# Residual stream kept turned by a reflection, with the normalisation computed inside the stages that make the stream

## What is computed

```
h = tokenizer(x)                                        # spectral features, one hidden layer, normalised
h = h + neighbourhood_attention(layernorm(h))
h = h + mixture_of_experts(layernorm(h))                # 8 experts, best 2 of them; itself residual: out = tokens + ...
h = h + decayed_attention(layernorm(h))
h = h + soft_experts(layernorm(h))                      # routing weights from mean over the batch of layernorm(h)
layernorm(h) = (h - mean(h)) / sqrt(var(h) + 1e-5)      # over the 64 channels of a token
```

## Time and profile before

| | before |
|---|---|
| median of 3 runs | 1049.62 us |
| the profiled execution | 1048.99 us, of which the span from first to last instruction is 1047.2 us |
| PE busy | 936.4 us (89%) |
| DVE busy | 583.4 us (56%) |
| ACT busy | 596.8 us (57%) |
| POOL busy | 174.8 us (17%) |
| DMA | 17.15 MB, mean 16 GB/s |
| mean granted TensorE clock | 0.967 of full speed |

### The profile page before, as it was taken

The page is one execution under the profiler, slowest core; times in us unless marked ns, Lnnn a source line. Parts: engine busy times, 40 slices in busy tenths (PEclk is TensorE's granted clock), DMA queues, the critical chain, the costliest instruction groups (busy, mean ns, idle before and its releaser), DMA issues. The chain is left out here.

```text
span 1047.2 us, 29479 instructions
## 1 busy us (share of the span) xinstructions
PE 936.4 (89%) x12388; PEld 447.7 (43%) x12388; DVE 583.4 (56%) x797; ACT 596.8 (57%) x822; POOL 174.8 (17%) x209
## 2 busy tenths in 40 slices
PE   3987969999999998864999999979999789999998
PEld 2331436667666766321222222337774422222222
DVE  3655346677676766246766755337874334444443
ACT  2998957676667676662444444662226545555543
POOL 1214131313131311034000000001113470000000
PEclk9998989999999999986999999989999899999999
DMA  2210000000000000000000000012210011211110
GB/s 53 28 27 0 1 2 4 5 4 4 4 4 5 4 4 4 2 1 0 1 2 1 1 1 1 1 30 52 52 32 1 0 31 41 58 45 42 41 41 31
DMA packets 27512, 17.15 MB, mean 16 GB/s; under 512 B 18753, under 2 KB 23010, under 8 KB 27394
## 3 DMA queue, kind: packets, MB, share of 16 engines
q1 hardware_dynamic: 26626, 14.16, 5.8%
q10 hardware_dynamic: 768, 1.23, 0.4%
HBM read 2.80 MB, written 4.19 MB: 7 GB/s over the span
## 5 line engine op out<-in xcount | busy, mean ns | idle before, releaser
L1585 DVE SCALAR_TENSOR_TENSOR se_a<-se_p,cols,z 128x1024 f32<-128x1024 f32 x64 | 82.2, 1284 | 118.9 <-PE se_p L1528 118.9
L1563 ACT ACTIVATE se_a<-se_p,cols 128x512 f32<-128x512 f32 x128 | 92.6, 773 | 79.8 <-PE se_p L1518 79.8
L1141 ACT ACTIVATE me_g<-me_p,cols 128x1024 f32<-128x1024 f32 x64 | 71.3, 1114 | 83.5 <-PE me_p L1095 83.4
L1232 DVE TENSOR_TENSOR me_gw<-me_pc,me_g 128x1024 f32<-128x1024 f32 x64 | 78.4, 1224 | 62.5 <-PE me_pc L1107 56.5
L991 DVE TENSOR_REDUCE na_rowmax<-na_ps 128x16 f32<-128x1024 f32 x64 | 78.0, 1219 | 54.0 <-PE na_ps L887 54.0
L801 POOL TENSOR_TENSOR z<-na_k,const 128x512 f32<-128x512 f32 x64 | 64.6, 1040 | 221.9 <-ACT na_k L940 221.9
L740 DVE TENSOR_TENSOR z<-ln_cen,ln_rstd 128x512 f32 (+1 forms) x64 | 44.3, 692 | 82.3 <-ACT ln_rstd L730 82.3
L896 PE MATMUL na_pt<-const,na_e 128*128 128x128 f32 x512 | 69.1, 278 | 14.2 <-ACT na_e L963 13.0
L994 DVE TENSOR_TENSOR na_e<-na_ps,na_rowmax 128x1024 f32<-128x1024 f32 x64 | 78.4, 1225 | 2.2
L1518 PE MATMUL se_p<-z,f_w 64*64 64x512 f32 x256 | 70.6, 624 | 4.0 <-DMA se_zswap<-z 4.0
L703 PE MATMUL ln_cen<-h,const 128*128 (+1 forms) x128 | 66.8, 610 | 6.4 <-DVEq L446 6.4
(11 more groups left out here) (222 smaller groups left out, 1538.7 us busy)
## 6 DMA issues: line engine op xcount, KB each, us to landing
da_zswap<-z SPq DMA_DIRECT2D x32, 128.0 KB, 2.3
se_zswap<-z SPq DMA_DIRECT2D x32, 128.0 KB, 2.4
out<-se_rows SPq DMA_DIRECT2D x16, 256.0 KB, 2.1
const<-in_const ACTq DMA_DIRECT2D x1, 720.5 KB, 4.7
f_w<-in_L_ffn_W SPq DMA_DIRECT2D x4, 128.0 KB
const<-in_const ACTq DMA_DIRECT2D x1, 448.0 KB, 3.7
moe_w<-in_L_ffn_w SPq DMA_DIRECT2D x2, 128.0 KB
raw<-in_L_ffn_b SPq DMA_DIRECT2D x12, 2.0 KB
```

Source lines behind the costliest of these rows:

```text
L1141: nc.scalar.activation(g[at.k % 2][:], p_1[:], ACT.Gelu, bias=col(s, "moe_b1", ep)).then_inc(s_g, 1)
L1232: nc.vector.tensor_tensor(gw[at.k % 2][:], p_c[:], g[at.k % 2][:], ALU.mult).then_inc(s_gw, 1)
L1563: ins = nc.scalar.activation(a1[at.k % 2][:, e2, :], p_1[at.k % 2][:, e2, :], ACT.Relu, scale=col(s, "f1_g1", 2 * ep + e2), bias=col(s, "f ...
L1585: nc.vector.scalar_tensor_tensor(out=a2[at.k % 2][:], in0=p_2[:], scalar=col(s, "f1_be2", ep), in1=s.f1_w[:, ep, :].unsqueeze(1).broadcast ...
```

## The change

The stream is kept multiplied by a fixed reflection (a Householder matrix `house`, its own inverse) that maps the mean direction of the 64 channels to channel 0. In that basis, to subtract the mean is to set channel 0 (partitions 0 and 64) to zero, and the variance is the sum of the squares of the other 63 channels over 64. All weights that read or write the stream are multiplied by the reflection once, in `spectral_norm` and `tokenizer_output` (house matmuls for those that read it, `turn_rows` on VectorE, with operations of up to 128x1088, for those that write it), and the last transposes of `soft_experts` become matmuls with `house`.

The four `layer_norm` blocks are gone. For each pair GpSimd squares the stream (`square`). For every four pairs TensorE makes their variances with 4 matmuls of 32 columns into one bank (`variance`), and ScalarE makes Ln and Exp of that bank once, so that one row of 512 deviations per sequence stands in a partition of `s.rstd`. SP copies each such row to 63 partitions of `s.bc` by DMA (`spread`: two DMAs per pair, each reading one partition 63 times, 2 KB each), and GpSimd multiplies (`scaled`). There are 4 buffers `s.bc`, so a `spread` waits for the `scaled` of four pairs before. This work is put in the stage that makes the stream, but for the tokenizer, whose copies and products lie at the start of `neighbourhood_attention`, and for pairs 12 to 15 of each stage, whose copies and products lie at the start of the next block. In the mixture of experts the Ln and Exp of the first 12 pairs are done at once, after pair 11, and their products by GpSimd after pairs 13, 14 and 15. In `soft_router` 16 matmuls of 32 columns over `s.z` take the place of GpSimd's sum. The memsets of the window buffers move to GpSimd in `spectral_norm`.

The diff, cut to its core:

```diff
+    w = np.full(D, D ** -0.5)
+    w[0] -= 1.0
+    w *= np.sqrt(2.0) / np.linalg.norm(w)
+    c["house"] = np.kron(np.eye(2), np.eye(D) - np.outer(w, w))
+    c["reflect"] = np.broadcast_to(w, (128, D))
+    c["others"] = np.zeros((128, 38))
+    c["others"][1:D, 6] = c["others"][D + 1:, 7] = 1.0 / D
...
+    s.sq, s.bc = [[sb(f"n_{x}{k}", [128, T]) for k in range(4)] for x in ("sq", "bc")]
+    s.rstd = sb("n_rstd", [128, NP // 4, T])
...
+def square(nc, s, p):
+
+    return nc.gpsimd.tensor_tensor(s.sq[p % 4][:], row(s.h, p), row(s.h, p), ALU.mult)
+
+
+def variance(nc, s, n, bank, start=True, stop=True):
+
+    at = CONST_AT["others"][0] + 6 - 2 * n
+    for j in range(4):
+        mm = nc.tensor.matmul(bank[32 * j:32 * j + 32, :], s.const[:, at:at + 32], s.sq[j][:], start=start, stop=stop, skip_group_check=True)
+    return mm
+
+
+def spread(sp, s, p, tile):
+
+    for b in range(2):
+        r = 32 * (p % 4) + 2 * (p // 4) + b
+        sp.dma_start(s.bc[p % 4][64 * b + 1:64 * b + 64, :], s.rstd[r:r + 1, tile, :].unsqueeze(1).broadcast_to([1, D - 1, T])).then_inc(s.n_bc[p % 4], 16)
+
+
+def scaled(eng, s, p):
+
+    return eng.tensor_tensor(row(s.z, p), row(s.h, p), s.bc[p % 4][:], ALU.mult)
...
+            def squares(at):
+                p = at.n
+                pool.wait_ge(s_h, done(p))
+                if p >= 4:
+                    pool.wait_ge(s.n_var, quad(0, p // 4 - 1))
+                square(nc, s, p).then_inc(s.n_sq, 1)
+
+            unrolled(NP, 4, (0, squares))
+            pool.wait_ge(s_turned, 2 * TURNED)
+            derive_turned(nc, s, step)
...
+            def before(at):
+                if at.n < NP // 2:
+                    for p in (2 * at.n, 2 * at.n + 1):
+                        pool.wait_ge(s.n_bc[p % 4], spread_done(0, p))
+                        scaled(nc.gpsimd, s, p).then_inc(s.n_z, 1)
+
+            def after(at):
+                p = at.n
+                pool.wait_ge(s_h, done(p))
+                if p >= 4:
+                    pool.wait_ge(s.n_var, quad(1, p // 4 - 1))
+                square(nc, s, p).then_inc(s.n_sq, 1)
+                if p >= 4:
+                    pool.wait_ge(s.n_bc[p % 4], spread_done(1, p - 4))
+                    scaled(nc.gpsimd, s, p - 4).then_inc(s.n_z, 1)
+
+            unrolled(NP, 2, (5, before), (0, after), (4, keys_by_head))
+
+        @block.sync
+        def _(sp):
+            for p in range(NP):
+                sp.wait_ge(s.n_rstd, quad(0, p // 4))
+                if p >= 4:
+                    sp.wait_ge(s.n_z, nth(0, p - 4))
+                spread(sp, s, p, 0)
+            for p in range(NP - 4):
+                sp.wait_ge(s.n_rstd, quad(1, p // 4))
+                sp.wait_ge(s.n_z, nth(1, p - 4))
+                spread(sp, s, p, p // 4)
...
+            def spreads(at):
+                if at.n % 8 == 7:
+                    n = at.n // 8
+                    te.wait_ge(s.n_sq, nth(1, 4 * n + 3))
+                    te.wait_ge(s_otd, done(min(4 * n + 4, NP - 1)))
+                    variance(nc, s, n, p_m).then_inc(s.n_var, 1)
+
+            unrolled(TURNS, 2, (4, scores), (4, even_values), (6, queries),
+                     (3, transposes(1)), (3, values(0)), (6, keys), (4, odd_values),
+                     (4, transposes(0)), (3, values(1)), (1, project), (2, turn), (0, spreads))
...
+            def deviations(at):
+                if at.n % 8 == 7:
+                    n = at.n // 8
+                    sc.wait_ge(s.n_var, quad(1, n))
+                    sc.wait_ge(s.n_z, nth(0, NP - 1))
+                    nc.scalar.activation(s.rstd[:, n, :], p_m[:], ACT.Ln, bias=s.eps[:]).then_inc(s.n_ln, 1)
+                    sc.wait_ge(s.n_ln, 2 + n)
+                    nc.scalar.activation(s.rstd[:, n, :], s.rstd[:, n, :], ACT.Exp, scale=-0.5).then_inc(s.n_rstd, 1)
+
+            unrolled(TURNS, 2, (4, fetch_even_values), (6, fetch_queries), (3, fetch(1)), (4, exponential(0)),
+                     (6, fetch_keys), (4, fetch_odd_values), (4, exponential(1)), (4, fetch(0)), (2, fetch_output), (0, deviations))
...
+            for p in range(NP - 4, NP):
+                pool.wait_ge(s.n_bc[p % 4], spread_done(1, p))
+                scaled(nc.gpsimd, s, p).then_inc(s.n_z, 1)
+            pool.wait_ge(s.n_z, nth(1, NP - 1))
 
             def tokens(at):
                 nc.gpsimd.tensor_tensor(row(s.h, at.n), row(s.h, at.n), row(s.z, at.n), ALU.add).then_inc(s_hz, 1)
 
-            unrolled(NP, 2, (0, tokens))
+            def after(at):
+                p = at.n
+                pool.wait_ge(s_h, done(p))
+                if p >= 4:
+                    pool.wait_ge(s.n_var, quad(2, p // 4 - 1))
+                square(nc, s, p).then_inc(s.n_sq, 1)
+                if p >= 13:
+                    for m in range(4 * (p - 13), 4 * (p - 13) + 4):
+                        pool.wait_ge(s.n_bc[m % 4], spread_done(2, m))
+                        scaled(nc.gpsimd, s, m).then_inc(s.n_z, 1)
+
+            unrolled(NP, 2, (2, tokens), (0, after))
...
+            def deviations(at):
+                if at.k == 14:
+                    n = at.of(16)
+                    sc.wait_ge(s.n_var, quad(2, n))
+                    sc.wait_ge(s.n_z, nth(1, 4 * n + 3))
+                    nc.scalar.activation(s.rstd[:, n, :], p_r[:], ACT.Copy).then_inc(s_copied, 1)
+                    if n >= 2:
+                        own = slice(0, 3) if n == 2 else slice(3, 4)
+                        sc.wait_ge(s_copied, done(n))
+                        nc.scalar.activation(s.rstd[:, own, :], s.rstd[:, own, :], ACT.Ln, bias=s.eps[:]).then_inc(s.n_ln, 1)
+                        sc.wait_ge(s.n_ln, 6 + n - 2)
+                        nc.scalar.activation(s.rstd[:, own, :], s.rstd[:, own, :], ACT.Exp, scale=-0.5).then_inc(s.n_rstd, 3 if n == 2 else 1)
+
+            unrolled(EP * NP, 16, (4, gelu), (6, fetch), (20, router), (0, deviations))
...
+            def normal(p):
+                sp.wait_ge(s.n_rstd, quad(3, p // 4))
+                sp.wait_ge(s.n_z, nth(3, p - 4))
+                spread(sp, s, p, p // 4)
+
+            def after(at):
+                if at.n >= 5:
+                    normal(at.n - 5)
+
+            for p in range(NP - 4, NP):
+                sp.wait_ge(s.n_rstd, quad(2, p // 4))
+                sp.wait_ge(s.n_z, nth(2, p - 4))
+                spread(sp, s, p, p // 4)
+            unrolled(NP, 2, (3, fetch), (0, after))
+            normal(NP - 5)
...
+                if at.n >= 5:
+                    te.wait_ge(s.n_rstd, quad(3, (at.n - 5) // 4))
...
-            unrolled(NP, 2, (0, scores), (1, project), (0, outputs))
+            def spreads(n, last):
+                te.wait_ge(s_h, done(last))
+                te.wait_ge(s.n_sq, nth(3, 4 * n + 3))
+                variance(nc, s, n, p_y).then_inc(s.n_var, 1)
+
+            def after(at):
+                if at.n >= 5 and at.n % 4 == 1:
+                    spreads((at.n - 5) // 4, at.n - 1)
+
+            unrolled(NP, 2, (0, scores), (1, project), (0, after), (0, outputs))
+            spreads(NP // 4 - 1, NP - 1)
...
+        LAST = range(NP - 4, NP)
+
+        @block.sync
+        def _(sp):
+            for p in LAST:
+                sp.wait_ge(s.n_rstd, quad(3, p // 4))
+                sp.wait_ge(s.n_z, nth(3, p - 4))
+                spread(sp, s, p, p // 4)
+
+        @block.gpsimd
+        def _(pool):
+            for p in LAST[0::2]:
+                pool.wait_ge(s.n_bc[p % 4], spread_done(3, p))
+                scaled(nc.gpsimd, s, p).then_inc(s_z, 1)
...
+            for p in range(NP):
+                if p == LAST[0]:
+                    te.wait_ge(s_z, 4)
+                mm = nc.tensor.matmul(p_sums[32 * (p % 4):32 * (p % 4) + 32, :], s.f1_wr, row(s.z, p), start=(p < 4), stop=(p >= NP - 4),
+                                      skip_group_check=True)
+            mm.then_inc(s_p, 1)
```

More of the change, by code:

```diff
@@ L38 @@
 ROUTES = 32
+W_OUT = 17
 KW, DIL = 31, 2
@@ L234, in later_loads @@
         loads.append((s.f1_wo[hf, :, :], a["L1_ffn_Wo"].rearrange("(p two) h d -> two h p d", two=2)[e2]))
-        loads.append((experts(s.raw_bo[n:n + 1, :], EP), a["L1_ffn_bo"].rearrange("(p two) d -> two p d", two=2)[e2:e2 + 1]))
+        loads.append((s.raw_bo[n:n + 1, :, :], a["L1_ffn_bo"].rearrange("(p two) d -> two p d", two=2)[e2:e2 + 1]))
         for pair in range(2):
@@ L616, in tokenizer_output @@
         g = [ctx.enter_context(nc.sbuf_tensor(f"to_g{k}", [128, 2, T], F32)) for k in range(4)]
+        tmp = ctx.enter_context(nc.sbuf_tensor("to_tmp", [128, W_OUT, D], F32))
+        total = ctx.enter_context(nc.sbuf_tensor("to_total", [128, W_OUT + 1], F32))
         y = [ctx.enter_context(nc.psum_tensor(f"to_y{k}", [128, T], F32)) for k in range(4)]
-        p_scale, p_bias = [ctx.enter_context(nc.psum_tensor("to_" + x, [128, 512], F32)) for x in ("scale", "bias")]
```

(46 more changed lines are left out.)

336 lines of the change are left out of this document (188 added, 148 removed).

## The result

The changed kernel takes **1269.97 us** (median of 4 runs, 1263.44 to 1277.08) against 1049.61 us for the kernel before on the same chip: ratio **1.211** (95% interval 1.206 to 1.216), slower. I had forecast 1194 with a range up to 1265. The profiled execution of it took 1277.08 us, of which 1275.1 are the span: 83.2 us more than the span of 1191.9 that I had summed up.

The account below looks back on a forecast made before the run. It took TensorE as busy nearly throughout the working stages, with four normalisation gaps between. Delays, mostly queued copies, put the router 144.9 us later: span 1047.2 + 144.9 - 0.2 = 1191.9, plus 1.8, forecast 1194; range 1170 to 1265, 980 to 1265 with the fast rival.

Parts of the forecast that it names:

- Which engine, which way: Whole kernel: slower 0.67, faster 0.32, within 0.2% 0.01, with block ends waiting for queued copies.
- The copy's price: Each spread: 4.46 us, a pair 8.9, at 28.9 GB/s per group of eight partitions; this case's chance 0.60.
- 17.8 us against about 18: just hidden: Neighbourhood attention after first scores: copies for two pairs take 17.8 us per pair computed in about 18, so hidden.
- The last transposes as matmuls: nothing, same shape and count: End of soft_experts: replacing the last transposes with matmuls was to cost nothing.
- 2.7 each for three: Decayed attention: outputs waits for Ln and Exp sharing its bank, 2.7 us at each of three stops, 8 in all.
- two table loads ... some 5: Mixture of experts after pair 11: Ln, Exp and two table loads stall the loop some 5 us, within 9.5.
- The predicted stall of the first residual behind `tokens`: Mixture of experts: tokens(0) ends at 501.9, first residual wants it at 492.9, so VectorE stands 9 us.
- Rival 1: Copies: a spread is as quick as a swapped copy, giving 992 us, faster; chance 0.30.
- The point of the change of sign: Copies: near 2.35 us per copy, 4.7 per pair; below it the kernel is faster, above it slower.
- Rival 2: Copies: one partition gives only what one engine draws, 21.6 GB/s, 12 us per pair, 1354 us; chance 0.06.

Follow-up runs that it names:

- e1: The changed kernel with each copy reading 63 partitions once instead of one partition 63 times, output not the reference's; 1035.45 us (ratio 0.987).
- e9: e3 with its three source partitions as neighbours inside one aligned group of eight instead of 8 apart; 1117.24 us (ratio 1.065).
- e11: e9 with the second sequence's rows moved by one, so each copy reads three partitions inside four aligned ones; 1133.59 us (ratio 1.081).
- e5: The kernel before plus unneeded copies of one row to 63 rows in the neighbourhood attention and mixture of experts; 1091.54 us (ratio 1.040).
- e6: e5 with each unneeded copy reading 63 partitions once, same count and bytes; 1050.90 us (ratio 1.001).
- e10: e5 with each unneeded copy writing 64 rows from one partition instead of 63; 1159.84 us (ratio 1.105).
- e4: The changed kernel with the last matmuls with house made transposes again, output left reflected; 1248.89 us in one execution, 1279.61 in the profiled one.
- e7: e3 with the stream turned back in soft_router and the last matmuls transposes again; 1035.37 us (ratio 0.986).
- e3: The changed kernel with each copy reading three partitions, 8 apart, 21 times each, output the reference's; 1058.82 us (ratio 1.0095).
- e8: e7 with ScalarE preloading one table for Ln and Exp in the decayed attention and mixture of experts; 1021.05 us (ratio 0.973).

## Why the prediction was wrong

**Which engine, which way: right.** Slower was the likeliest side (0.67), for the reason given: a copy from one partition is slow, copies stand in line in one queue, and the block ends wait for them. The first copy was issued at 118.87 (said: the block begins at 120.8), first scores at 163.0 (163.7), mixture's first expert matmul 20.3 us behind the last residual (20.2), the tail of the mixture 104.6 (106.9), the decayed attention's first matmul 40.1 us behind the end of the mixture's last product (38.6). The chain of these is all that the forecast of the copies rested on, and it holds within 8 us of 371.

**The copy's price: size near, reason wrong.** 4.06 us for 4.46. The rate belongs to the single partition (e1 with the same engines, e9 and e11 with 54 GB/s out of one group), not to a group of eight.

**"17.8 us against about 18: just hidden": this step failed, 48 us.** For the products it was true: after the start GpSimd waits at most 5.3 us at a time for a copy. But I looked for cover only among those who wait for the data. The copies also hold the DMA engines, and TensorE halts for packets of its program that come late (e5, e6, e10). The stretch grew by 55.0 us, of which I had 7: the halts, 39.4 us against 3.3, are 36 of it, and TensorE's busy time, 279.2 against 263.7 at a clock of 0.93 for 0.99, is 15.5 more. 3.2 of these are the variances, which with their waits of 4.4 us cost the 7 forecast. The row for it stood in the page of before, the instruction queue of 97 packets; the prediction gives it no term.

**"The last transposes as matmuls: nothing, same shape and count": failed, 24.7 us.** Same shape, but not the same work per instruction (e4: 22.3; e7 against e3: 23.4).

**Decayed attention, "2.7 each for three": mis-sized, 12.4 us.** Each stop costs about 6 us: in e3, with quicker copies, `outputs` steps by 10.0 and 7.1 us around it where it steps by 5.6 else; three times 3.2 more than I had is 9.6 of the 12.4. I had counted table loads in the mixture and forgotten them here; 10.7 to 12.4 us went with them in e8, over half of it as busy time of TensorE at the lower clock, which the prediction did not count either. What the swapped copies lose by queueing behind spreads was in the sum with 12.4 us (114.3 less 93.9 and 8), and the stretch is 14.1 longer than in e3 (125.9 against 111.8).

**Mixture, "two table loads ... some 5": mis-sized, 5 us.** There are three, the third to bring Gelu back:

```profile
676.29 1.07 PE L462 MATMUL me_pr<-n_sq,const 128*32 128x512 f32 x8
677.42 0.60 ACT L1293 ACTIVATE n_rstd<-me_pr 128x512 f32<-128x512 f32 x1 [1.32 <-PE me_pr L462]
678.03 1.28 ACT L1297 ACT_TABLE_LOAD   x1
679.33 1.57 ACT L1297 ACTIVATE n_rstd<-n_rstd,eps 128x1536 f32<-128x1536 f32 x1
680.98 1.28 ACT L1299 ACT_TABLE_LOAD   x1
682.27 1.48 ACT L1299 ACTIVATE n_rstd<-n_rstd 128x1536 f32<-128x1536 f32 x1
683.77 1.28 ACT L1280 ACT_TABLE_LOAD   x1
...
685.07 1.11 ACT L1280 ACTIVATE me_g<-me_p,cols 128x1024 f32<-128x1024 f32 x1
```

From the variance to the next Gelu it is 8.8 us. The predicted stall of the first residual behind `tokens`, 9 us, came: at 549.23 it has waited 8.54 us for GpSimd's sum.

**The rivals.** Rival 1, copies as quick as swapped ones, is what e1 makes true by other means: 1035, not 992, for the same missing terms (24 for the last matmuls, 11 in the decayed attention). Even so it is a little faster than before. The point of the change of sign, 2.35 us per copy, was set too high: e3 with 1.7 us is at 1059, slower. Rival 2 fell: one partition gives more than the 21.6 GB/s assumed. My range counted only errors of the copies; all four misses lay in terms that I had given one value and no bounds.

## What to carry to other kernels

A copy that repeats one partition is slow for its source and costs others too: it holds DMA engines for long at few bytes, and an engine with thousands of small instructions then halts for its program. Let the step before write the row into several partitions (here free, the matmul's columns were empty), count over how many DMA engines the copy's shape then goes, and read "busy share high, GB/s low" as a warning for every engine. Price each replaced instruction by its own row, transposes and table loads included, even if its shape is the same.

## What the hardware showed that I had not expected

- One SBUF partition read by DMA gave 32 GB/s (8.1 us per pair of copies) to 9 engines; three neighbours gave 54 to 3 engines, and it made no difference to the pace whether they lay within four aligned rows or only within eight (4.8 us per pair both).
- The shape of a copy set its engines: 63 rows from one or from 63 partitions went over 9, 64 rows over 16, three partitions read 21 times each over 3, seven read nine times each over 7. Three engines carried 74 GB/s at 84 ns per packet of 2 KB, more than 9 engines got from one partition.
- 63 rows from one partition (DMA share 0.46) and 64 (0.88) moved at the same 30 to 32 GB/s; the wider spread was the worse one for TensorE, 94.6 us of halts against 39.4.
- The instruction queue brought one 16 KB packet each 4.3 us in a stage of 29 matmuls per us, and TensorE's halts ended 1.1 to 1.6 us after a late one had landed. Where a stage had 977 matmuls in 177 us, the same copies cost it 0.5 us.
- A 128x128 fp32 product has two records where a transpose of that shape has one, and keeps TensorE busy for 533 ns against 186 (34.1 / 64 and 11.9 / 64).
